# The add that ends the rope, on VectorE instead of GpSimd

## The reference

```python
x = x + attention(layernorm(x), ctx, pos)
x = x + experts(layernorm(x))

# in attention:
q = (xn @ Wq).reshape(b, n, 32, 8);  k, v = split(ctx @ Wkv)
q = rope(q, pos);  k = rope(k, pos)
w = softmax(einsum('bqhd,bkhd->bhqk', q, k) * scale)
out = einsum('bhqk,bkhd->bqhd', w, v).reshape(b, n, 256) @ Wout + bout

# rope, for each pair (x1, x2) of a head, with the angle of its position:
out = stack([x1 * cos - x2 * sin, x1 * sin + x2 * cos])

# experts: two best of 8 scores, y += w_e * (silu(x @ W1[e].T) * (x @ W2[e].T)) @ W3[e].T
```

## Time and profile before

| | us |
|---|---|
| median of 3 executions | 647.45 (642.0 to 647.96) |
| the profiled execution | 645.48 |
| its span, first to last instruction | 643.7 |

### The profile page before, as it was taken

How to read it: one execution, slowest core, us unless ns; L and a number is a source line. 1 busy time by engine, 2 the same in 40 slices (tenths; PEclk the granted TensorE clock), 3 DMA queues, 4 the chain that set the end, 5 groups by cost and what they waited for, 6 DMA issues and landing times.

```text
span 643.7 us, 22842 instructions
## 1 busy us (share of the span) xinstructions
PE 521.7 (81%) x7955; PEld 406.2 (63%) x7956; DVE 421.8 (66%) x1145; ACT 312.7 (49%) x806; POOL 367.1 (57%) x578
## 2 busy tenths in 40 slices
PE   2779998888989899898988878849999999999300
PEld 1546666566666566565666556628999999999200
DVE  6346877777777677776876655755555655556386
ACT  2346666566665666666566544524333433333000
POOL 5656668677786776878777434231555555555300
PEclk9769999999999999999999979657999999999755
DMA  4100322131121211112110011442333333332498
GB/s 98 28 24 17 94 66 83 49 94 53 49 71 40 61 51 41 54 32 61 33 50 20 22 35 35 124 123 65 114 119 114 112 107 112 102 121 76 128 374 306
DMA packets 53192, 54.04 MB, mean 84 GB/s; under 512 B 10853, under 2 KB 48879, under 8 KB 53104
## 3 DMA queue, kind: packets, MB, share of 16 engines
q1 hardware_dynamic: 41696, 31.29, 17.5%
q0 software_dynamic: 6480, 16.82, 7.2%
q10 hardware_dynamic: 4928, 4.72, 2.2%
HBM read 29.31 MB, written 23.90 MB: 83 GB/s over the span
## 4 chain that ended last, share of the span: by engine, by line
PE 47%; issue 17%; POOL 14%; DVE 13%; DMA 5%; ACT 1%; SPq 1%; POOLq 0%; ACTq 0%; DVEq 0%
PE logit_banks L1287 11%; POOL mid L558 8%; PE logit_banks L1305 6%; DVE negmax L647 6%; PE logit_banks L1104 6%; POOL routed_rows L568 5%; PE logit_banks L1125 5%; PE logit_banks L1133 4%; DMA mid<-result_rows 3%; PE bank L1265 2%; PE bank L1296 2%; DVE rden L654 2%; PE bank L1115 1%; PE logit_banks L1217 1%; PE bank L1071 1%
## 5 line engine op out<-in xcount | busy, mean ns | idle before, releaser
L596 POOL DMA_INDIRECT result_rows<-w12a,blk_dest x71 | 69.4, 977 | 88.6 <-DVE w12a L865 78.6
L568 POOL DMA_INDIRECT routed_rows<-xs,slots x64 | 65.7, 1026 | 88.1 <-PE bank L1192 48.0
L647 DVE TENSOR_REDUCE negmax<-logit_banks 128x16 f32<-128x1024 f32 x64 | 75.3, 1218 | 36.4 <-PE logit_banks L1104 36.4
L949 ACT ACTIVATE late<-logit_banks 128x1024 f32<-128x1024 f32 x64 | 65.5, 1025 | 57.6 <-PE logit_banks L1133 56.8
L558 POOL TENSOR_TENSOR mid<-mid,mask 128x512 f32<-128x512 f32 x64 | 65.3, 1046 | 15.1 <-ACT mid L930 14.5
L1031 ACT ACTIVATE act_h<-logit_banks 128x176 f32<-128x176 f32 x71 | 22.5, 317 | 98.0 <-PE logit_banks L1287 98.0
L633 DVE TENSOR_TENSOR rope_a<-bank,cos_t 128x512 f32<-128x512 f32 x32 | 22.1, 692 | 68.5 <-PE bank L1073 68.5
L850 DVE TENSOR_TENSOR gated<-act_h,logit_banks 128x176 f32<-128x176 f32 x71 | 24.0, 338 | 65.2 <-ACT act_h L1031 65.2
L654 DVE RECIPROCAL rden<-bank 128x256 f32<-128x256 f32 x32 | 55.9, 1748 | 4.9 <-PE bank L1157 4.7
L1287 PE MATMUL logit_banks<-w_hi,x_hi 128*128 x142 | 48.4, 341 | 8.3 <-DVE x_lo L860 7.4
L936 ACT ACTIVATE late<-mid,mask 128x256 f32<-128x256 f32 x128 | 54.2, 497 | 0.0
(11 more groups left out here) (161 smaller groups left out, 1381.1 us busy)
## 6 DMA issues: line engine op xcount, KB each, us to landing
xb<-routed_rows SPq DMA_DIRECT2D x71, 128.5 KB, 2.1
mid<-result_rows SPq DMA_DIRECT2D x32, 256.0 KB, 5.0
x_sb<-in_x_dram SPq DMA_DIRECT2D x32, 128.0 KB, 2.1
out_dram<-late ACTq DMA_DIRECT2D x16, 256.0 KB, 5.1
ctx_sb<-in_ctx_dram SPq DMA_DIRECT2D x32, 64.0 KB, 2.0
mid<-mT SPq DMA_DIRECT2D x128, 4.0 KB
w12a<-in_L_ffn_W_dram SPq DMA_DIRECT2D x2, 1024.0 KB, 6.3
routed_rows<-pad_row SPq DMA_DIRECT2D x11, 128.5 KB, 3.3
```

The lines of the kernel that those rows point to most:

```text
L568: nc.gpsimd.indirect_dma_start(routed[:, :], bass.IndirectOffsetOnAxis(ap=slots[:, t.slot(TR), k:k + 1], axis=0), xs[:, t.slot(TR), k, :], ...
L596: nc.gpsimd.indirect_dma_start(results[:, :], bass.IndirectOffsetOnAxis(ap=blk_dest[:, b.slot(RB):b.slot(RB) + 1], axis=0), y_sb[:, b.slot ...
L647: V.tensor_reduce(negmax[:, t.par, 16 * half:16 * half + 16], ps_s[:, 1024 * half:1024 * half + 1024].rearrange("p (h k) -> p h k", k=N), ...
L949: S.activation(pT[:, 1024 * half:1024 * half + 1024], ps_s[:, 1024 * half:1024 * half + 1024], ACT.Exp, scale=SCALE).then_inc(exp_done, 1)
```

## The change

`rotate` leaves the GpSimd program and stands in the VectorE program. Its instruction, its operands and its two waits are the same; it is issued by the other engine. In GpSimd's turn it was the last stage; in VectorE's turn it stands right behind `rope` of the same tile, ahead of `residual`.

```diff
@@ gpsimd @@
-            def rotate(t):
-                pool.wait_ge(rope_done, t.n + 1)
-                wait_past(pool, kqT_done, t.n)
-                nc.gpsimd.tensor_tensor(rot[:], rope_a[:], rope_b[:], ALU.add).then_inc(rot_done, 1)
-
@@ gpsimd, body @@
                 do(mask_keys, t.plus(2))
-                do(rotate, t.plus(3))
@@ vector @@
                 ins.then_inc(rope_done, 1)
+
+            def rotate(t):
+                dve.wait_ge(rope_done, t.n + 1)
+                wait_past(dve, kqT_done, t.n)
+                V.tensor_tensor(rot[:], rope_a[:], rope_b[:], ALU.add).then_inc(rot_done, 1)
@@ vector, body @@
                 do(rope, t.plus(3))
+                do(rotate, t.plus(3))
                 do(residual, t.plus(-1))
```

## The result

The changed kernel takes 661.55 us (median of 4 runs, 658.35 to 664.38) against 644.73 us of the kernel before, run beside it: a ratio of 1.021, 95% interval 1.016 to 1.027. The profiled execution took 661.52 us, with a span of 659.8 us against 643.7: 16.1 us more. The change makes the kernel slower, clear of the noise; whether by more or less than 2% these runs leave open.

The account below looks back on a forecast made before the run. Every turn was taken to pass through GpSimd from the rank to the end of the masks. 645.48 us (profiled) + 12.5 steady + 2.2 start = 660.2, or 662.2 from the median; forecast 661, range 647 to 667 us.

Parts of the forecast that it names:

- The sum: Whole kernel: profiled 645.48 us plus 12.5 in the steady part and 2.2 at the start, 660.2; forecast 661.
- Removing the add from GpSimd: GpSimd, steady part: 25 adds of 1.273 us go, ahead of 1.68 us of waiting for TensorE's rank; worth 0.
- The add's own length: VectorE: the uncontended add of 128x512 float32 with two SBUF inputs takes 0.69 us, at the lower end 0.552.
- The two collide: Steady turns: VectorE's add meets GpSimd's first mask, and an instruction of one engine waits for one of the other.
- four places of the trace: Places in the earlier trace said to show GpSimd and VectorE disturbing each other, such as L697 ending with L541.
- The add gets in between the masks: Steady turns: the add waits for the first mask only and makes the second 0.5 us late; 25 turns, 12.5 us.
- the first rival: Steady turns: the add waits behind both masks, maxima start 0.68 us late; 19.2 us more, 664.7 us; chance 0.15.
- The price of the rival: Both masks first: statistics end at 192.71 and the maxima start 0.68 us late in each of 25 turns.
- The start: Before the steady part: in three turns the maxima directly follow L625, so the add costs 3 x 0.69; put at 2.2 us.
- The cover holds everything: Steady part: second mask not held up, statistics end 0.32 us before the maxima; only the start costs, 647.7 us; chance 0.19.
- faster: Steady part: x1's scalars come earlier, L529 near 191.5 instead of 192.06, each turn gains 0.5 us; 635 us; chance 0.04.
- More than one collision: Steady part: L546 may also hold up L691, L697 and the rank, another 0.3 us a turn; 668 us; chance 0.04.

Follow-up runs that it names:

- the pair of extra instructions: Kernel before plus one extra VectorE multiplication out of PSUM: ratio 1.007; kernel before plus one extra VectorE add of two SBUF tiles: ratio 1.068.
- with the gap: Changed kernel with GpSimd's second mask waiting for the end of the first: ratio 1.031.
- changed kernel with early masks: Changed kernel with the two masks moved ahead of the scatter in GpSimd's turn: ratio 1.004 to the kernel before.
- kernel before with early masks: Kernel before, add still on GpSimd, with the two masks moved ahead of the scatter in GpSimd's turn: ratio 0.995.
- VectorE's extra add: Kernel before plus an extra VectorE add of the same two SBUF tiles into a spare tile, behind the rope: 691.58 us, ratio 1.068.

## Why the prediction was right, and where it was not

- *The sum.* 661 was forecast with +12.5 us in the steady part and +2.2 at the start; measured are +12.2, +2.4 and 1.4 behind them, for which the sum had nothing. The turn was put at 11.8 us and is 11.78. That the number is this close is luck, as the next points show: a wrong order of the collision, and a start whose reason is partly another.
- *Removing the add from GpSimd is worth nothing.* Right in the result. One sign of it was wrong: GpSimd's idle time ahead of the scatter did not rise by over 1 us, it is 1.60 us (1.68 in the earlier trace rows). The freed time appears elsewhere, as 1.85 us of waiting for L676 ahead of L529, because the statistics stand behind the add. That L529 is not late either held for a free add only.
- *The add's own length*, 0.69: measured 0.691.
- *The two collide.* Right; the pair of extra instructions shows it, 1.007 against 1.068. (The prediction speaks of four places of the trace and names three: L697, L687 and L523.)
- *The add gets in between the masks.* Wrong. This is the step that failed: what happened is the first rival, both masks first, which I had given 0.15, with all three of its signs: masks of 1.05, an add of 1.82 us, no idle time of VectorE ahead of the maxima. None of the 25 steady turns went as forecast. I had read from L697 that VectorE gets in between two GpSimd instructions even if the second is dispatched already. In the steady turns the add does not, except where the second mask is held back until the first has ended; then the turn looks as I had forecast it (0.83 us, 1.39 us, VectorE idle for 0.84). L697 stands behind L541, which reads one tensor where a mask reads two, and needs 8 elements; which of these matters was not tried, and two adds at the start of other runs did get in.
- *The price of the rival.* I had 0.68 us a turn for it, measured are 0.49. The add ends 0.56 us behind the masks, as worked out (0.54). But the 1.42 us for residual and statistics were counted from the residual's start, 0.08 before the rope's end; behind the add they end 1.34 us later. The maxima start 0.08 us before the statistics end, as L625 and L647 do in the earlier trace rows, and take 0.04 less. These three make up the 0.2 us between 0.68 and 0.49. That the order forecast was put at 0.5 us and the one that came costs 0.49 is why the number came out in spite of the wrong step. The lower end of my 0.5, 0.35, counts some 0.2 us at the start of a GpSimd instruction as free of reading; no run shows that. Where the add did get in, the second mask took 0.34 us more (1.39, with the gap) or 0.44 more (1.49, at the start).
- *The start.* The size was right, the reason only in part. Until the maxima at 32.21 and 44.94 the changed kernel is ahead of the kernel before (32.42, 45.66). Its first add ends 0.7 us earlier, but its granted clock is higher there too, 0.83 and 0.73 against 0.66 and 0.61; which of the two gives the lead is not shown. Then the turn from there takes 12.19 us at a granted clock of 0.86, where that of before took 9.88 at 1.00. At 1.00 the same turn takes 10.62 us in the changed kernel with early masks and 9.88 in the kernel before with early masks. So of the 2.3 us some 0.7 go with the add, as I had it for this turn, and some 1.6 with the clock, which the sum did not have.
- *The cover holds everything* and *faster*: neither appeared. *More than one collision*: L696 rose to 0.331 us in the median (0.252 in the earlier trace rows), and TensorE waited for it in two turns, 1.6 us in all.

For one instruction against one, the first to start was served first: VectorE's extra add had its 0.69 us, and GpSimd's add, 0.05 us behind it, took 1.78 instead of 1.27. For GpSimd instructions that stand back to back, the recorded starts did not give the order: VectorE's add at 195.26 started ahead of the second mask, at 195.48, and still waited for it (1.82 us).

## What to carry to other kernels

Before moving an elementwise instruction from GpSimd to VectorE, look at where its inputs lie and at what GpSimd does at that moment: two SBUF inputs beside a GpSimd instruction that reads SBUF cost a wait on one side here (1.82 us instead of 0.69 for VectorE's add, or 1.78 instead of 1.27 for GpSimd's), whatever cover the two engines showed in busy time. Look for the place by the other engine's idle stretches, not by the data's readiness: here the same add cost 2% right behind its inputs, and nothing measurable behind the next turn's maxima. And where GpSimd runs instructions back to back, reckon with a wait for the whole run of them (here 1.82 us recorded beside two, 2.80 to 3.05 beside three), and put few things behind the waiting instruction.

## What the runs showed of the hardware that was not expected

- In the steady turns VectorE's add waited for the end of all GpSimd instructions that overlap in the record (two masks: 1.82 us, two masks and an add: 2.80 to 3.05), and for the first only where 0.07 us lay between them (0.83). Twice, at the start of a run, it got in between two overlapping masks (1.30 and 1.31 us, the second mask 1.49).
- A recorded length contains the waiting: an add of 0.69 us was recorded with 0.69, 0.83, 1.82 and 2.92.
- The scatter's DMA issues on GpSimd did not hold up a VectorE add with two SBUF inputs: 0.69 us beside them, and the issues themselves took 1.10 and 0.96 (1.09 and 0.96 in the earlier trace rows).
- Kernels with the same median turn can differ by a percent: the changed kernel and the one with the gap both have 11.78 us, and ratios of 1.021 and 1.031, with three and seven of 24 turns at a granted clock of 0.87.
